# The sums over the state index: four 64x64 products for two units, y banks by row halves

## What is computed

```python
def step(h, inp):
    dt_t, B_t, C_t, u_t = inp
    dA = jnp.exp(dt_t[:, :, None] * A)
    h = h * dA + (dt_t * u_t)[:, :, None] * B_t[:, None, :]
    y = jnp.einsum('bdn,bn->bd', h, C_t)          # the sum over the state index n
    return (h, y)
...
y = jnp.transpose(ys, (1, 0, 2)) + u * D_param    # the skip
y = y * jax.nn.silu(z)                            # the gate
return jnp.einsum('bsd,ed->bse', y, out_proj_w)
```

## Time and profile before

| | us |
|---|---|
| median of 3 runs | 2156.11 |
| lowest, highest | 2149.99, 2160.99 |
| span of the profiled execution | 2153.9 |
| PE, DVE busy in it | 1887.8, 1935.2 |
| ACT, POOL busy in it | 1719.8, 1821.9 |
| sums (L1648) busy on PE, 1536 records | 775.3 |

### The profile page before, as it was taken

How to read it: one execution, slowest core, us unless ns; L and a number is a source line. 1 busy time by engine, 2 the same in 40 slices (tenths; PEclk the granted TensorE clock), 3 DMA queues, 4 the chain that set the end, 5 groups by cost and what they waited for, 6 DMA issues and landing times. The chain is left out here.

```text
span 2153.9 us, 22717 instructions
## 1 busy us (share of the span) xinstructions
PE 1887.8 (88%) x5980; PEld 975.5 (45%) x5980; DVE 1935.2 (90%) x2022; ACT 1719.8 (80%) x3125; POOL 1821.9 (85%) x906
## 2 busy tenths in 40 slices
PE   8968789899888989899898989899899988778798
PEld 7533334445354544445454443535445443324356
DVE  5479999999999999999999998999999999899963
ACT  2387788888889888898989888888989987677652
POOL 0088998989898998989899997989989898989950
PEclk9889989999999999999999999999999999899999
DMA  6056665656466575646656675555556666555630
GB/s 247 1 170 174 176 195 150 196 168 185 138 178 176 165 207 166 196 146 180 173 160 187 176 209 155 167 176 164 171 165 195 173 181 179 174 166 176 192 93 20
DMA packets 170543, 358.77 MB, mean 167 GB/s; under 512 B 19544, under 2 KB 27952, under 8 KB 161712
## 3 DMA queue, kind: packets, MB, share of 16 engines
q1 hardware_dynamic: 151958, 279.32, 39.8%
q0 software_dynamic: 9216, 67.11, 15.3%
q10 hardware_dynamic: 9242, 10.89, 1.5%
HBM read 284.85 MB, written 5.29 MB: 135 GB/s over the span
## 5 line engine op out<-in xcount | busy, mean ns | idle before, releaser
L765 POOL TENSOR_TENSOR state<-state,c_rows 128x1024 f32<-128x1024 f32 x512 | 1214.9, 2410 | 139.2 <-DVE state L1328 95.8
L1648 PE MATMUL bank<-state,const_sb 128*128 128x512 f32 x1536 | 775.3, 620 | 111.2 <-POOL state L765 63.7
L1328 DVE TENSOR_TENSOR_SCAN state<-decay,mix_banks 128x512 f32<-128x512 f32 x640 | 753.2, 1207 | 31.5 <-ACT decay L1044 14.5
L1325 DVE TENSOR_TENSOR_SCAN state<-mix_banks,state 128x512 f32<-128x512 f32 x384 | 450.4, 1204 | 30.5 <-ACT mix_banks L1028 19.7
L1648 PEld LDWEIGHTS bank<-state,const_sb 128*128 128x128 f32 x1536 | 282.2, 196 | 423.9 <-issue 252.3
L756 POOL TENSOR_TENSOR state<-kept,b_rows 128x1024 f32<-128x1024 f32 x192 | 469.1, 2443 | 3.4 <-DMA b_rows<-flat_rows 1.7
L1044 ACT ACTIVATE decay<-kept,ssm_pack 128x512 f32<-128x512 f32 x640 | 435.3, 711 | 1.0
L1318 DVE TENSOR_TENSOR mix_banks<-kept,mix_banks 128x1024 f32<-128x1024 f32 x320 | 392.8, 1227 | 28.9 <-ACT mix_banks L1036 19.6
L1028 ACT ACTIVATE mix_banks<-kept,ssm_pack 128x512 f32<-128x512 f32 x384 | 259.5, 683 | 115.7 <-DVE state L1328 101.2
L1544 PE MATMUL bank<-kept,ssm_pack 128*128 128x512 f32 x512 | 244.2, 613 | 25.9 <-DVE kept L1277 8.4
L1036 ACT ACTIVATE mix_banks<-b_rows 128x512 f32<-128x512 f32 x320 | 187.8, 591 | 51.2 <-DVE state L1328 27.6
(11 more groups left out here) (198 smaller groups left out, 2208.7 us busy)
## 6 DMA issues: line engine op xcount, KB each, us to landing
b_rows<-flat_rows SPq DMA_DIRECT2D x512, 256.0 KB, 3.9
c_rows<-flat_rows SPq DMA_DIRECT2D x512, 256.0 KB, 3.6
state<-state POOLq DMA_DIRECT2D x64, 1024.0 KB, 9.7
out<-x_res ACTq DMA_DIRECT2D x8, 512.0 KB, 7.4
ssm_pack<-ssm_pack SPq DMA_DIRECT2D x2, 2035.0 KB, 13.2
x_next<-x ACTq DMA_DIRECT2D x6, 512.0 KB, 7.2
state<-ada_w SPq DMA_DIRECT2D x1, 1536.0 KB, 12.3
kept<-ada_w SPq DMA_DIRECT2D x1, 1536.0 KB, 15.1
```

The lines of the kernel that those rows point to most:

```text
L765: pool.tensor_tensor(st, st, by_pair(c_rows[:, row % ROWS]), ALU.mult).then_inc(m_prod, 1)
L1325: ins = dve.tensor_tensor_scan(st, mixed, st, 0.0, ALU.mult, ALU.add)
L1328: ins = dve.tensor_tensor_scan(st, decay[:, nth(g) % DECAYS], mixed, 0.0, ALU.mult, ALU.add)
L1648: pe.matmul(y_banks[c2][:], ident, state[:, g % STATES], start=False, stop=(g == in_bank[-1])).then_inc(m_sum, 1)
```

## The change

Two units of a pair are summed together, by four products. Product (k, c2) takes the rows k of chunk c2 (64 partitions of the state tile) as the moving operand and a 64x64 identity as the weights, and writes to the partitions `to` (half c2) of bank k. So bank k now holds the upper (k = 0) or lower (k = 1) 64 channels of both chunks of the half, one above the other. The skip is split the same way. One increment of `m_sum` stands for a pair, and the order of sums goes by pairs at the tick of the pair's odd unit. The two gates of a half are at one tick (5) and take bank k with the k-th permuted chunk of silu(z). To match, the z columns of w_in and the rows of w_out are permuted on the host when the inputs are packed. State tiles, folds, product rows and all other tables stay.

```diff
--- before.py
+++ after.py
@@ -22,6 +22,7 @@
 SCANS = 2 * B
 PAIRS = B // 2
 SLOTS = 4
+ROW_HALVES = (slice(0, P // 2), slice(P // 2, P))
 
 SUM_LAG = 5
 BANKS, DECAYS, STATES, ROWS = 3, 7, 20, 4
@@ -247,20 +248,19 @@
 def sum_ticks():
 
     at = {}
-    for g in range(ALL_UNITS):
+    for g in range(0, ALL_UNITS, HC):
         if not fold_from(g):
-            at.setdefault(g + (FOLDED_LAG if fold_into(g) else SUM_LAG), []).append(g)
+            at.setdefault(g + 1 + (FOLDED_LAG if fold_into(g) else SUM_LAG), []).append(g)
     return at
 
 
 SUMS_AT = sum_ticks()
 SUM_ORDER = [g for tick in sorted(SUMS_AT) for g in SUMS_AT[tick]]
-SUM_COUNT = {g: n for n, g in enumerate(SUM_ORDER, 1)}
-BANK_SUMS = {}
-for unit_ in SUM_ORDER:
-    BANK_SUMS.setdefault((unit_ // HALF_UNITS, unit_ % HC), []).append(unit_)
-GATE_TICKS = tuple(max(t for t, units in SUMS_AT.items() for k in units if k < HALF_UNITS and k % HC == c2) + 1 - HALF_UNITS
-                   for c2 in range(HC))
+SUM_COUNT = {g + k: n for n, g in enumerate(SUM_ORDER, 1) for k in range(HC)}
+HALF_SUMS = {}
+for pair_ in SUM_ORDER:
+    HALF_SUMS.setdefault(pair_ // HALF_UNITS, []).append(pair_)
+GATE_TICK = max(t for t, pairs in SUMS_AT.items() for k in pairs if k < HALF_UNITS) + 1 - HALF_UNITS
 
 
 def prep_fill(pi, what):
@@ -1328,16 +1328,16 @@
                     ins = dve.tensor_tensor_scan(st, decay[:, nth(g) % DECAYS], mixed, 0.0, ALU.mult, ALU.add)
                 ins.then_inc(m_scan, 1)
 
-            def gate(si, half, c2):
+            def gate(si, half, k):
 
                 layer, s = scan_of(si)
-                c = half * HC + c2
+                c = half * HC + k
                 if c == 0:
                     taken(dve, prep_fill(si, "z2"))
                     taken(dve, prep_fill(si, "z3"))
-                dve.wait_ge(m_sum, SUM_COUNT[BANK_SUMS[si * HALVES + half, c2][-1]])
+                dve.wait_ge(m_sum, SUM_COUNT[HALF_SUMS[si * HALVES + half][-1]])
                 taken(dve, prep_fill(si, f"z{c}"))
-                dve.tensor_tensor(u[s][:, c, :], y_banks[c2][:], zh[s][:, c, :], ALU.mult).then_inc(m_gate, 1)
+                dve.tensor_tensor(u[s][:, c, :], y_banks[k][:], zh[s][:, c, :], ALU.mult).then_inc(m_gate, 1)
 
             def unit(g, part):
                 if part == 0:
@@ -1347,10 +1347,10 @@
                     return
                 if is_unit(g):
                     scan(g)
-                for c2, tick in enumerate(GATE_TICKS):
-                    if g % HALF_UNITS == tick and is_unit(g - HALF_UNITS):
-                        si, half, *_ = split(g - HALF_UNITS)
-                        gate(si, half, c2)
+                if g % HALF_UNITS == GATE_TICK and is_unit(g - HALF_UNITS):
+                    si, half, *_ = split(g - HALF_UNITS)
+                    for k in range(HC):
+                        gate(si, half, k)
 
             run_batches(setup, attention, before, tail, after, unit)
 
@@ -1626,26 +1626,32 @@
                                           per_token("gather", h, permute, spread, 1))
                 yield from w.to("end")
 
-            def skip(si, half, c2):
+            def skip(si, half):
                 layer, s = scan_of(si)
-                c = half * HC + c2
-                if c < HC:
+                if half == 0:
                     pe.wait_ge(s_gate_nat, 2)
                     pe.wait_ge(s_mod[3], 1)
                     pe.wait_ge(s_skip, 2)
-                past(pe, m_gate, si * CH + c - HC + 1)
-                pe.wait_ge(p_u, si * CH + c + 1)
-                pe.matmul(y_banks[c2][:], skip_diag[layer][:, c, :], u[s][:, c, :], start=True, stop=False)
+                past(pe, m_gate, si * CH + half * HC)
+                pe.wait_ge(p_u, si * CH + half * HC + HC)
+                for k, rows in enumerate(ROW_HALVES):
+                    for c2, to in enumerate(ROW_HALVES):
+                        c = half * HC + c2
+                        pe.matmul(y_banks[k][to, :], skip_diag[layer][rows, c, rows], u[s][rows, c, :], start=True, stop=False)
 
             def sum_up(g):
-                si, half, n, c2, c = split(g)
-                in_bank = BANK_SUMS[g // HALF_UNITS, c2]
-                if g == in_bank[0]:
-                    skip(si, half, c2)
+                si, half, *_ = split(g)
+                in_half = HALF_SUMS[g // HALF_UNITS]
+                if g == in_half[0]:
+                    skip(si, half)
                 pe.wait_ge(m_prod, g // HC + 1)
                 for n in fold_into(g):
                     pe.wait_ge(m_fold[n], 16 * (g // HALF_UNITS) + 16)
-                pe.matmul(y_banks[c2][:], ident, state[:, g % STATES], start=False, stop=(g == in_bank[-1])).then_inc(m_sum, 1)
+                for k, rows in enumerate(ROW_HALVES):
+                    for c2, to in enumerate(ROW_HALVES):
+                        ins = pe.matmul(y_banks[k][to, :], ident[rows, rows], state[rows, (g + c2) % STATES],
+                                        start=False, stop=(g == in_half[-1]))
+                ins.then_inc(m_sum, 1)
 
             def unit(g, part):
                 for j in SUMS_AT.get(g, ())[part::2]:
@@ -1707,6 +1713,7 @@
         film_w[layer] = give(f"film_w_{layer}", ew)
         att_rows[layer] = [give(f"att_row_{layer}_{k}", r) for k, r in enumerate((g("bq"), g("bv"), ob, g("bk")))]
     gate_rows = []
+    by_half = np.arange(DI).reshape(HALVES, HC, 2, P // 2).transpose(0, 2, 1, 3).reshape(DI)
     for layer in SSM:
         g = lambda s: a[f"L{layer}_cond_{s}"]
         if layer == 1:
@@ -1715,6 +1722,8 @@
         else:
             w_in, w_x, w_dt, w_out, ada = (g(s) for s in ("W_in", "W_xp", "W_dt", "W_out", "W_ada"))
             conv, dt_b, ng, nb, ab = g("conv_w")[:, 0, :], g("b_dt"), g("gamma"), g("beta"), g("b_ada")
+        w_in = np.concatenate([w_in[:, :DI], w_in[:, DI:][:, by_half]], axis=1)
+        w_out = w_out[by_half]
         parts = dict(w_in=chunks(w_in), w_x=chunks(w_x), w_dt=rows_of(w_dt), w_out=chunks(w_out), conv_w=chunks(conv),
                      conv_b=cols(g("conv_b")), dt_b=cols(dt_b), a_log=chunks(g("A_log")), d_skip=cols(g("D_param")),
                      norm_g=cols(ng), norm_b=cols(nb), ada_b=cols(ab))
```

## The result

The changed kernel is slower: median 2209.53 us (2203.83 to 2215.19, 4 runs) against 2157.64 us of before, ratio 1.0238, 95% interval 1.021 to 1.0266. The forecast was 2138 us, range 2114 to 2206.

A forecast was written before the change was run, and what follows sets the result against it. The prediction took DVE, busy 1753.0 of 1850 us in the scans, as nearly full, with PE's lateness costing 39.6 us. Span 2153.9 - 26 (relief) + 8 (clock) = 2135.9 us, as median 2138 us; range 2114 to 2206.

The forecast's parts named there:

- The overlap: On PE, a pair's four 64x64 products run side by side: 0.86 us a pair, 357 us of PE saved.
- The visit: On PE, going to the 64-row shape and back costs 0.40 us; about 262 visits, 105 us.
- Weight loads: On PE, a pair's eight weight loads take about 0.96 us, partly pulled forward; some 20 us in all.
- Rivals two and three: Two: a product's two records delay each other, 2191 us, chance 0.28. Three: products run one after another, 2720 us, 0.11.
- rival two: On PE, a pair costs four slots, 1.71 us, as before, plus 105 us of visits; 2191 us, chance 0.28.
- signs of being wrong: Distance as forecast but DVE still waits as long, or sums gain and the granted clock falls below 0.9.
- Ticks and gates, at nothing: Even sums one tick later and both gates at one tick add no wait, so cost 0 us.
- The clock: PE's granted clock in the scans falls from 0.97 to 0.93, taking back 8 us (bounds 0 and 26).
- what reaches the end: Of the 39.6 us that PE's lateness costs, two thirds, 26 us, come off the span.
- hidden: Rival one: products run side by side but the time does not move; 2156 us, 2146 to 2166, chance 0.17.
- The ceiling: In the scans PE's lateness costs 15.3 + 20.3 + 4.0 = 39.6 us, the most a PE relief can win.
- 300 us of air: Counted by record starts, PE has work for about 1550 of the scans' 1850 us, leaving 300 us.

The follow-up runs named there:

- e1: Changed kernel's order kept, but each pair summed by two full 128x128 products instead of four small ones; 2190.7 us, ratio 1.0152 to the kernel before.
- g1: f2's order (pair sums at the even unit's tick, gates at tick 5) with two full 128x128 products a pair; 2170.0 us, ratio 1.0057.
- f1: e1 with both gates two ticks later in DVE's order (tick 7 instead of 5), nothing else; 2203.4 us, ratio 1.0212.
- f4: Kernel before, in its own order, with even units' sums cut to 8 of 512 columns except each bank's last; 2188.7 us, ratio 1.0141.
- e3: e1 with the even unit's sum left out in every pair except the last one of a half; 2211.9 us, ratio 1.0254.
- e2: e1 with each unit's sum split into two products of 128 rows and 64 columns; 2203.8 us, ratio 1.0216.
- g3: f2 with four zero products of 64x64 and 256 columns put ahead of each pair's wait for POOL's product; 2171.3 us, ratio 1.0063.
- g4: Kernel before with one zero product of 128 columns ahead of the wait of each even unit's sum; 2175.2 us, ratio 1.0072.
- g2: f2 with the same four 64x64 products with zero weights ahead of each pair, behind the wait; 2194.1 us, ratio 1.0163.
- h1: g1 with one tiny 64x64 product of zero weights, 8 columns, ahead of each pair's two full products; 2213.4 us, ratio 1.0255.
- f2: Changed kernel with the pair sums one tick earlier, at the even unit's tick, and the gates left at tick 5; 2183.6 us, ratio 1.0116.
- h2: f2 with the pair sums done two pairs at a time, at the later pair's tick; 2194.2 us, ratio 1.0175.
- e4: Changed kernel with one full 128x128 product of zero weights, 512 columns, ahead of each pair's four products; 2219.9 us, ratio 1.0288.
- f3: Changed kernel with each pair's four 64x64 products preceded by the same four with zero weights; 2211.4 us, ratio 1.0244.
- h3: h2 with one group of four zero products of 512 columns ahead of each second pair's wait; 2216.4 us, ratio 1.0273.

## Why the prediction was wrong, point by point

**The overlap was right.** I took all four side by side, 0.86 us a pair and 0.9 to 1.1 us for the eight records; measured 1.02. The visit was put at 0.40 us and is 0.36; there are 271 of them, not 262. Weight loads I had put at about 0.96 us a pair; the eight are listed within 0.21 us. PE busy in the scans was forecast at 1414 us and is 1437.5. Rivals two and three fell with it: rival two's range, 2175 to 2215 us, holds the result, but by luck: its mechanism, the two records in each other's way, did not occur. Two of the prediction's own signs of being wrong came true: the sums gained and the clock fell below 0.9, and with the distance as forecast DVE waited longer (34.1 us for PE and 66.8 for ACT, where under 8 and under 35 were forecast).

**"Ticks and gates, at nothing" failed, and is the largest error.** The order alone costs 33 us (e1, 1.5%), 21 of them by the one tick (g1 to e1). I had looked for new waits on a semaphore and found none; true, but the sums moved closer to what stood right behind them. The gates waited only 2.3 us in the scans before because a tick of about 1.9 us (1958.9 us for 1024 units) was just enough; over the whole execution the 64 gates wait 24.2 us with the pairs at the odd unit's tick (e1) and 4.7 us with them a tick earlier (g1). A small wait at a tight place is no slack. Behind the gates I named the next scan and left out the out projection (L1602), which f1 showed waiting 32.0 us.

**The clock: right sign, wrong size.** I took 8 us off for a fall to 0.93, from the last stretch. It fell to 0.89: 484 us at the lower level instead of the 14% (about 300 us) that I had reckoned. The step that failed is "what reaches the end": the relief was put at 26 us of gain, and the clock at 8 us of it. With work alone reduced the net is a loss: +30 us in f4, +21 in e3, and +6 from e2 to the changed kernel, which the intervals can't tell from zero. The prediction's upper bound for the clock (26 us, "hidden") had the clock giving back all of the gain, not more. A reason that the rows suggest and no run separates: the relief falls on the sums, which wait 100 us for POOL and the fold anyway, while the lower clock falls on everything, the projections that ACT and DVE wait for included.
The Trainium skill ("TensorE: Matmul & The Clock Gate", Part 1) says that the throttled state is the default and that activity lifts it; the runs agree: 0.97 with 1632 us busy in the scans, 0.93 with 1560 (g3), 0.89 with 1438. The amount of work is not all of it: f4 has 0.89 with 1529 us. The tails of its 704 tiny records are in that, but counted by starts, as in the prediction, f4 has 1431 us and g3 1444 at 0.93. Nor did the last stretch of the kernel before foretell it: it had 0.93 with PE busy 77%, the changed kernel has 0.89 with 78%.

**The ceiling counted one way only.** That PE's lateness cost 39.6 us bounded what could be won; nothing bounded what could be lost. The runs with added work at a clock of 0.95 and more say how much of PE's time reaches the end: g4 16 of 81 us, e1 to e2 13 of 98 (271 x 0.36), g1 to g2 24 of 93 (259 visits), g1 to h1 43 of 154: 13% to 28%, where the visits in us are estimates from the 0.36 and 0.40 us of single ones. With 300 us of air by my count of starts I had priced the visits as mere load.

**The sum as it came out:** 2157.6, + 12 (lumps and joined gates, g1), + 21 (the late tick, e1), + 13 (visits, e2), + 6 (half the slots, with the clock from 0.96 to 0.89) = 2209.6 us. The first two together are 1.0152, the first three 1.0216, all 1.0238. The split follows the one way in which I added the parts; on f2's order they weigh differently (24 for the visits from g1 to g2, then 10 back from g2 to f2), and the 6 us lie within the intervals.

Left open: the 12 us of g1, how much of the order's 33 us goes by way of the clock, whether later sums or longer lumps make h2 lose, and whether g3 gains over g2 by its place or by its smaller amount.

## What to carry to other kernels

Taking work from TensorE is no gain by itself: where other engines wait for its other products, ask what the granted clock does when the work is gone, and test it by leaving work out (f4) before building the real thing. In a fixed order one tick is a price: look at what stands directly behind the moved step on each engine, and read a wait of 2 us at such a place as the end of the slack. If work must be put back to hold the clock, try a small amount of it ahead of a wait: of the six kernels with added products of zeros (e4, f3, g2, g3, g4, h3) only g3 won time against the kernel that it was added to, though whether by the place or by the amount is not shown.

## What the runs showed of the hardware that I had not expected

- Float32 products on the four 64x64 parts of the array run side by side although each is two records: first records 6 to 7 ns apart, second ones together a slot later, 1.02 us for eight records instead of the 3.44 of eight slots. Column halves alone (128x64) do so in pairs: 1.87 us for eight.
- Eight 64x64 weight loads are listed within 0.21 us, those of 128x128 at 0.11 us apart (0.30 us for two in the earlier trace rows).
- Products with zero weights raise the granted clock (0.890 to 0.951 in f3).
